# Graph layer and ternary feed-forward on one core: a lighter first stage, and shared node columns added by TensorE

## What is computed

```
n  = layernorm(x)
s  = segment_sum(n[src], dst, 1250);  deg = segment_sum(1, dst, 1250)
h  = n @ W_self + (s / max(deg, 1)) @ W_neigh + b
h  = where(h >= 0, h, 0.01 * h)
x  = x + h / max(norm(h, axis=1), 1e-12)
wq = w with each group of 128 inputs as clip(round(w / scale), -1, 1) * scale, scale = mean|w| + 1e-5
m  = layernorm(x)
x  = x + (silu(m @ wq_gate.T) * (m @ wq_up.T)) @ wq_down.T
```

## Time and profile before

| | |
|---|---|
| three runs | 363.98, 365.71, 365.72 us; median 365.71 |
| profiled execution | 365.24 us, span 363.3 us, mean granted clock 0.987 |
| busy (share of the span) | PE 329.8 (91%), DVE 304.6 (84%), ACT 238.0 (66%), POOL 163.1 (45%) |
| stage one | to 121.98 us |
| stage two | 121.98 to about 177 us |
| stage three | from there to the end |

### The profile page before, as it was taken

One profiled execution on the slowest core, in us unless ns is written; L12 is line 12 of the kernel. 1 busy time (PEld: TensorE's weight loads), 2 busy tenths in 40 slices (PEclk: granted clock), 3 DMA queues, 4 the chain that ended last, 5 costly groups with the idle time before them and its releaser, 6 DMA issues.

```text
span 363.3 us, 5834 instructions
## 1 busy us (share of the span) xinstructions
PE 329.8 (91%) x1623; PEld 249.6 (69%) x1623; DVE 304.6 (84%) x789; ACT 238.0 (66%) x637; POOL 163.1 (45%) x223
## 2 busy tenths in 40 slices
PE   1997879899999999999687999999999999999992
PEld 0443335554545578777476898989899898889991
DVE  3569999899889248999696998999999989999994
ACT  2155958899787136774656768668777678676670
POOL 7000000110010590110003466888788787799992
PEclk9999999999999999999988999999999999999998
DMA  7961322233232001200000000000000000000215
GB/s 226 291 159 33 86 58 78 68 88 87 59 82 79 3 3 35 74 22 2 0 1 2 0 3 0 3 0 0 2 3 2 0 0 3 0 3 0 73 44 169
DMA packets 9412, 16.69 MB, mean 46 GB/s; under 512 B 1062, under 2 KB 1886, under 8 KB 9378
## 3 DMA queue, kind: packets, MB, share of 16 engines
q1 hardware_dynamic: 9300, 16.21, 15.9%
q10 hardware_dynamic: 78, 0.08, 0.1%
HBM read 13.73 MB, written 2.56 MB: 45 GB/s over the span
## 4 chain that ended last, share of the span: by engine, by line
PE 58%; DVE 26%; ACT 10%; issue 3%; POOL 1%; DVEq 0%; ACTq 0%; POOLq 0%
PE bank L1320 39%; PE bank L1208 7%; PE bank L1250 5%; DVE tq_gu L901 4%; DVE hot_dst L1005 3%; ACT mag_early L690 3%; DVE tq_d L901 2%; DVE hot_src L996 2%; ACT a_t L742 2%; DVE bn L1061 2%; ACT hot_src L675 2%; DVE x_sb L1058 2%; DVE z L1040 1%; PE bank L1232 1%; PE bank L1156 1%
## 5 line engine op out<-in xcount | busy, mean ns | idle before, releaser
L1320 PE MATMUL bank<-x_hi,t_gu 128*128 128x378 f32 (+1 forms) x264 | 96.9, 367 | 3.6 <-DVE x_lo L1075 2.8
L1320 PE MATMUL bank<-x_lo,t_gu 128*128 128x378 f32 (+1 forms) x264 | 95.5, 362 | 0.0
L1208 PE MATMUL bank<-w_sb,xnT 128*125 128x512 f32 x160 | 86.9, 632 | 4.8 <-ACT z L725 4.1
L1114 DVE SCALAR_TENSOR_TENSOR g_acc<-bank,nscale,g_acc 128x378 f32<-128x378 f32 (+1 forms) x99 | 64.3, 650 | 12.1 <-PE bank L1320 10.8
L612 POOL TENSOR_SCALAR thr<-absum 128x4 f32<-128x4 f32 (+1 forms) x34 | 10.7, 315 | 121.5 <-ACT mag_early L690 97.2
L1114 DVE SCALAR_TENSOR_TENSOR u_acc<-bank,nscale,u_acc 128x378 f32<-128x378 f32 (+1 forms) x99 | 64.1, 647 | 0.0
L633 POOL TENSOR_TENSOR acc<-acc,d_one 128x378 f32<-128x378 f32 (+1 forms) x58 | 60.9, 1052 | 0.1
L643 POOL TENSOR_TENSOR hh<-sg,u_acc 128x378 f32<-128x378 f32 (+1 forms) x32 | 35.1, 1098 | 57.4 <-ACT sg L830 57.3
L1320 PEld LDWEIGHTS bank<-x_hi,t_gu 128*128 128x128 f32 x264 | 51.1, 193 | 8.1 <-DVE x_lo L1075 3.5
L1320 PEld LDWEIGHTS bank<-x_lo,t_gu 128*128 128x128 f32 x264 | 51.0, 193 | 3.6
L1167 PEld LDWEIGHTS bank<-hot_dst,hot_src 128*125 128x125 bf16 x157 | 20.8, 137 | 42.0 <-DVE hot_dst L1005 23.0
(11 more groups left out here) (136 smaller groups left out, 558.5 us busy)
## 6 DMA issues: line engine op xcount, KB each, us to landing
raw<-in_L_ffn_w_gate SPq DMA_DIRECT2D x11, 256.0 KB, 2.7
raw<-in_L_ffn_w_up SPq DMA_DIRECT2D x11, 256.0 KB, 2.6
out_x<-x_sb SPq DMA_DIRECT2D x10, 224.0 KB
raw<-in_L_ffn_w_down SPq DMA_DIRECT2D x8, 256.0 KB, 2.7
x_sb<-in_x SPq DMA_DIRECT2D x1, 1344.0 KB
w_sb<-in_L_gnn_W_neigh SPq DMA_DIRECT2D x1, 1024.0 KB, 6.0
w_sb<-in_L_gnn_W_self SPq DMA_DIRECT2D x1, 1024.0 KB, 7.3
raw<-in_L_ffn_w_down SPq DMA_DIRECT2D x4, 192.0 KB, 2.3
```

The lines of the kernel that those rows point to most:

```text
L1114: nc.vector.scalar_tensor_tensor(out=to, in0=bank_of(u, what)[:, 0:w], scalar=nscale[:, j:j + 1], in1=to, op0=ALU.mult, op1=ALU.add).then_ ...
L1208: last = nc.tensor.matmul(to[0:TP, :], xnT[:, t, k * TP:(k + 1) * TP], w_sb[:, k, half * D:(half + 1) * D], start=k == 0, stop=k == KD - 1)
L1320: last = nc.tensor.matmul(to, w, parts[h], start=h == 0, stop=h == 1)
```

## The change

- Stage one holds 18 loads (72 jobs) instead of 25; the other 16 (60 jobs) stand in stage two: five before the first neighbour sum, then 4, 3, 2 and 2 after tiles 0 to 3 (`PHASE`, `late_jobs`). In stage one ACT's magnitudes begin four slots later than before, and DVE's signs come four slots after that.
- The joins go. ACT copies a block's 50 columns, and at a block's end PE adds the shared column: it waits for the copy of the block before (`block_out`), and multiplies that column of `a_t` by the identity into column 0 of the block. PE loads the 32 base columns into registers for it (before, DVE did that). The one join of the last block stays.
- The bias is added by PE: ones times the bias in two parts (high and rest), as a ninth product of z. POOL's additions go.
- From tile 2 on ACT, not DVE, normalizes the rows.
- ACT spreads the source numbers over 32 columns into a table of its own, and DVE's compare reads them four times. DVE makes the chunk tables two slots ahead.
- `x1_low` comes one tile earlier.

```diff
+    LOADS1 = 18
+    PHASE = [5, 4, 3, 2, 2, 0, 0, 0, 0, 0]
...
-        LOADS1 = 2 * NF + 3
...
-        def down_jobs(n):
-
-            lo, hi = (LOADS1 + max(0, min(NL, 3 * i // 2)) for i in (n, n + 1))
-            return range(load_end[lo - 1], load_end[hi - 1])
+        def late_jobs(n):
+
+            lo = LOADS1 + sum(PHASE[:n])
+            return range(load_end[lo - 1], load_end[lo + PHASE[n] - 1])
...
-            for t in range(NT):
-                pool.wait_ge(z_out, t + 1)
-                nc.gpsimd.tensor_tensor(z[:, t, :], z[:, t, :], bias_b[0:TP, :], ALU.add).then_inc(z_done, 1)
...
-                nc.scalar.activation(hot_src[:, b % SBS, 0:n, 0:TP],
-                                     src_lo[:, SB * b:SB * b + n, None].to_broadcast([P, n, TP]), ACT.Copy).then_inc(src_wide, 1)
+                nc.scalar.activation(src_rep[:, b % SBS, 0:n, :],
+                                     src_lo[:, SB * b:SB * b + n, None].to_broadcast([P, n, REP]), ACT.Copy).then_inc(src_wide, 1)
...
+                if i == 0 and 1 <= t and t + 1 < NT:
+                    act.wait_ge(shifted, 1 if t + 1 < LN_GROUPS[3][0] else 2)
+                    act.wait_ge(xn_T, t)
+                    nc.scalar.activation(xn[0:TP, (t + 1) % 2, :], x_sb[:, t + 1, :], ACT.Identity, bias=shift0[0:TP, t + 1:t + 2],
+                                         scale=rs[0:TP, t + 1:t + 2]).then_inc(normed, 1)
...
-                            to, cols = a_t[:, :, 1:N][:, :, bass.ds(bases[k], WIN - 1)], slice(1, WIN)
+                            to, cols = a_t[:, :, bass.ds(bases[k], WIN)], slice(0, WIN)
...
+            for j in late_jobs(0):
+                abs_of(j)
             for n in range(NT):
...
-                for j in down_jobs(n):
-                    abs_of(j)
+                if n < NT - 1:
+                    for j in late_jobs(n + 1):
+                        abs_of(j)
...
-                    for c in chunks_in(slot + 1):
+                    for c in chunks_in(slot + 2):
...
-                            nc.vector.tensor_tensor(hot_src[:, b % SBS, 0:n, 0:TP], iota[:, None, 0:TP].to_broadcast([P, n, TP]),
-                                                    hot_src[:, b % SBS, 0:n, 0:TP], ALU.is_equal)
+                            nc.vector.tensor_tensor(
+                                hot_src[:, b % SBS, 0:n, :].rearrange("p n (a r) -> p n a r", r=REP),
+                                iota[:, None, 0:P].rearrange("p n (a r) -> p n a r", r=REP).to_broadcast([P, n, P // REP, REP]),
+                                src_rep[:, b % SBS, 0:n, None, :].to_broadcast([P, n, P // REP, REP]), ALU.is_equal)
...
-                for k in blocks_ending(slot - 2):
-                    if k:
-                        join(k)
+                if NB - 1 in blocks_ending(slot - 2):
+                    join_last()
...
+            for j in late_jobs(0):
+                ternary_of(j)
             for n in range(NT):
                 neighbour_sum(n)
...
-                if n >= 4:
-                    x1_low(n - 4)
-                for j in down_jobs(n - 1):
-                    ternary_of(j)
+                if n >= 3:
+                    x1_low(n - 3)
+                if n < NT - 1:
+                    for j in late_jobs(n + 1):
+                        ternary_of(j)
...
+                if c == last_chunk[k] and 0 < k < NB - 1:
+                    pe.wait_ge(block_out, k)
+                    nc.tensor.matmul(bank[k % 3][0:TP, 0:NT * WIN].rearrange("p (s d) -> p s d", d=WIN)[:, :, 0:1],
+                                     ident[0:TP, 0:TP], a_t[:, :, bass.ds(bases[k], 1)].bitcast(F32),
+                                     start=False, stop=True, skip_group_check=True).then_inc(block_done, 1)
...
+                if half and k == KD - 1:
+                    if t == 0:
+                        pe.wait_ge(bias_set, 2)
+                    last = nc.tensor.matmul(to[0:TP, :], ones_r[0:33, 0:1].to_broadcast([33, TP]), bias_r[0:33, :],
+                                            start=False, stop=True)
```

More of the change, by code:

```diff
@@ L256, in chunk_used @@
             k = window(c)[0]
-            return (block_done, k + 1) if c == last_chunk[k] else (hot_used, c + 1 - k)
+            alone = k in (0, NB - 1) and c == last_chunk[k]
+            return (block_done, k + 1) if alone else (hot_used, c + 1 - (k > 0))
         def blocks_ending(slot):
@@ L552, in _ @@
             load_x(3)
-            sp.dma_start(bias_b[:, :], bias.rearrange("(a n) -> a n", a=1).to_broadcast([P, D])).then_inc(bias_in, 16)
+            sp.wait_ge(zeroed, 4)
+            for r in (0, 32):
+                sp.dma_start(bias_f[r:r + 1, :], bias.rearrange("(a n) -> a n", a=1)).then_inc(bias_in, 16)
             for l, (w, n) in enumerate(loads):
@@ L589, in _ @@
             nc.gpsimd.memset(a_t[:, :, LASTB:N].bitcast(F32), 0.0).then_inc(zeroed, 1)
+            nc.gpsimd.memset(bias_f[:], 0.0).then_inc(zeroed, 1)
             nc.gpsimd.memset(base_f[:, 0:1], 0.0).then_inc(zeroed, 1)
@@ L729, in _ @@
                 if slot < SLOTS:
-                    for j in jobs_in(slot, 6):
+                    for j in jobs_in(slot, 10):
                         abs_of(j)
@@ L896, in reciprocals, with shift0_of @@
                 dve.wait_ge(rstd, i + 1)
+            def shift0_of(i):
+                a, b = LN_GROUPS[i]
+                nc.vector.scalar_tensor_tensor(out=shift0[0:TP, a:b], in0=mv[0:TP, a:b, 0], scalar=-1.0, in1=rs[0:TP, a:b],
+                                               op0=ALU.mult, op1=ALU.mult).then_inc(shifted, 1)
             def ternary_of(j):
@@ L982, in _ @@
                     reciprocals(3)
-                if i == 0 and 1 <= t and t + 1 < NT:
-                    normalize(t + 1)
+                    shift0_of(3)
                 if i == 2 and 1 <= t <= NT:
@@ L1005, in _ @@
                         nc.vector.tensor_scalar(to, numbers, key[:, c:c + 1], None, ALU.is_equal).then_inc(hot_made, 1)
-                if slot == FIRST + 2:
-                    dve.wait_ge(prep, 9)
-                    _, bases = nc.values_load_multi_w_load_instructions(
-                        base_i[0:1, :], engines=[dve.engine], min_val=0, max_val=LASTB,
-                        skip_runtime_bounds_check_because="base_f is clamped to 0..LASTB on the chip")
-                for k in blocks_ending(slot - 2):
-                    if k:
-                        join(k)
+                if NB - 1 in blocks_ending(slot - 2):
+                    join_last()
                 if slot == CHECK:
@@ L1020, in _ @@
                     any_outside = dve.value_load(flag[0:1, 0:1])
-                for j in jobs_in(slot, 10):
+                for j in jobs_in(slot - 4, 10):
                     ternary_of(j)
@@ L1169, in add_chunk @@
                                  hot_dst[:, c % HOT, 0:NT * (hi - lo)].rearrange("p (s d) -> p s d", d=hi - lo),
-                                 start=c == first_chunk[k], stop=c == last_chunk[k],
-                                 skip_group_check=True).then_inc(block_done if c == last_chunk[k] else hot_used, 1)
+                                 start=c == first_chunk[k], stop=c == last_chunk[k] and k in (0, NB - 1),
+                                 skip_group_check=True).then_inc(chunk_used(c)[0], 1)
+                if c == last_chunk[k] and 0 < k < NB - 1:
[3 more added lines that the diff above has]
+                                     start=False, stop=True, skip_group_check=True).then_inc(block_done, 1)
             pe.wait_ge(const_done, 11)
@@ L1188, in _ @@
                     pe.wait_ge(w_self_in, 16)
+                if slot == FIRST + 2:
+                    pe.wait_ge(prep, 9)
+                    _, bases = nc.values_load_multi_w_load_instructions(
+                        base_i[0:1, :], engines=[pe.engine], min_val=0, max_val=LASTB,
+                        skip_runtime_bounds_check_because="base_f is clamped to 0..LASTB on the chip")
                 if slot == 1:
@@ L1208, in _ @@
                 last = nc.tensor.matmul(to[0:TP, :], xnT[:, t, k * TP:(k + 1) * TP], w_sb[:, k, half * D:(half + 1) * D],
-                                        start=k == 0, stop=k == KD - 1)
+                                        start=k == 0, stop=not half and k == KD - 1)
+                if half and k == KD - 1:
[3 more added lines that the diff above has]
+                                            start=False, stop=True)
                 if k == KD - 1:
```

83 lines of the change are left out of this document (44 added, 39 removed).

## The result

| | before | the change |
|---|---|---|
| median | 365.62 us (4 runs) | 381.39 us (4 runs: 380.40 to 382.00) |
| ratio | | 1.044, 95% interval 1.040 to 1.048 |
| profiled execution, span | 365.24, 363.3 us | 380.40, 378.2 us |
| first neighbour product (T) | 121.98 us | 122.98 us |
| from there to the last transposes of stage two | 54.68 us | 68.58 us |

The account below looks back on a forecast made before the run. The prediction took TensorE to be the bound in both stages: 365.2 us + 1.3 before T + 13.8 of stands in stage two + 0.4 for the clock = 380.7 us, about 4% slower, range 371 to 389.

Parts of the forecast that it names:

- What bounds the kernel: Both stages: TensorE is the bound; before T, lightening DVE or ACT can win at most 9.4 us.
- The waits of stage one: TensorE's waits for DVE's tables and ACT's copies of z before T: 8.4 of 9.4 us credited as won.
- register load: Before T, TensorE loads 32 bases into registers: 0.8 us more, ends 0.1 and 1.2.
- Identity products: Before T, 30 fp32 products on TensorE at 0.22 us each: 6.6 us more, ends 3 and 15.
- Bias products: Before T, ten products of 512 columns on TensorE at a neighbour product's pitch, 0.23 us: 2.3 us more.
- Sum before T: All stage-one terms together, -8.4 + 6.6 + 2.3 + 0.8: T comes 1.3 us later.
- Source table: DVE's compare in stage one, reading a run of 32 four times: 0.70 us for 1024 elements, today's rate.
- The chain of stage two: After T, magnitudes, thresholds and signs precede DVE's early sums: first transposes of normalized rows at T + 30.5, last about T + 68.5.
- The stands: Stage two, TensorE idle 0.6, 7.9, 3.5 and 3.0 us, less 1.2 of today's waits: 13.8 us more.
- The clock: Stage two, TensorE's clock at 0.50 for a tile or so after the 7.9 us stand: 0.4 us, ends 0 and 2.
- The x_lo step: Feed-forward products in stage two: x_lo one tile earlier wins nothing, since the fourth product needs the same x_lo.
- POOL's additions: Stage two: DVE waited 4.9 us for POOL's ten bias additions, but TensorE was busy then, so removing them wins nothing.

Follow-up runs that it names:

- k3: The change without its ten bias products, POOL adding the bias one tile at a time between its thresholds: 377.28 us, 1.035 of the kernel before.
- k1: The kernel before with only the change's job table, and POOL's bias additions set between its early thresholds: 378.21 us, 1.036 of the kernel before.
- k10: The kernel before with ACT normalization, source table of 8 columns, tables two slots ahead, signs two slots behind magnitudes: 361.22 us, 0.991 of the kernel before.
- k11: k10 with the early magnitudes starting four slots later, signs still two slots behind them: 360.73 us, 0.988 of the kernel before.
- k4: The change without the 30 identity products and TensorE's register load, DVE joining the shared columns as before: 378.64 us, 1.039 of the kernel before.
- k9: The change with the old job table, source table of 8 columns, early signs two slots behind magnitudes, x_lo one tile later: 370.69 us, 1.017.
- k7: The change with its 16 late loads spread flat, two after each of tiles 0 to 7: 384.31 us, 1.055 of the kernel before.
- k8: k7's flat table with DVE's signs one tile behind ACT's magnitudes: 374.93 us, 1.029 of the kernel before.
- k6: The change with the bias product's ones written out as 33 x 125 elements instead of one repeated column: 382.03 us, 1.047 of the kernel before.
- k2: The change with the job table of before (25 loads early) and a source table of 8 columns: 374.49 us, 1.026 of the kernel before.
- k5: The change with the old job table, joins on DVE, bias on POOL between thresholds, source table of 8 columns: 374.09 us, 1.027 of the kernel before.

## Why the prediction was right

- **What bounds the kernel.** Stage one: right. Each step that took products from TensorE moved T (k3 by 4.5 us from the first chunk product), and steps that only lighten DVE and ACT won less than the 9.4 us (k1 2.1, k10 2.9, k11 4.4).
- **The waits of stage one.** I credited 8.4 of the 9.4; all went. The register load was 0.6 (I took 0.8).
- **Identity products.** 0.14 to 0.19 by the starts of the slots, up to 0.20 by k4: some 0.16, 4.8 us, where I had 0.22 and 6.6.
- **Bias products: the term that failed.** "At the pitch of a neighbour product, 0.23", 2.3 us in all, was 0.56 and 5.6 us by the starts. The nearest row had the columns but not the place: this product follows an fp32 projection, not another of its kind.
- **Sum before T: right by luck.** With what was measured, -9.4 + 4.8 + 5.6 + 0.6 = +1.6; T moved +1.0; I had +1.3. The bias products were 3.3 us dearer than forecast; the identity products were 1.8, the waits 1.0 and the registers 0.2 cheaper, which cancels it to 0.3. A term was missing too: the new zeroing of the bias rows on POOL (5.84 to 6.36) was costed at nothing, but DVE's first normalization beside it grew by 0.46 us, in every run with the bias products, and TensorE's first transposes began at 7.97 instead of 7.50 (rows in the last section). The eight records of the start took 0.39 us less in the change's execution (6.10 us), so T hides it.
- **Source table.** 684 ns for 1024 elements, where I took 0.70.
- **The chain of stage two.** In us after T, forecast and measured: signs of the first group done 8.9 and 9.1, second sum 17.4 and 17.8, third sum 26.2 and 26.7, first transposes 30.5 and 31.0, last ones 68.5 and 68.6. DVE's signs waited 7.9 us for thresholds up to the third sum (some 7). That the table makes the loss is shown by k1 and k9. That the loss is waiting between engines is shown by k7 against k8 for the flat table; the change's own table was not run with a tile of lag, and for it the waits for thresholds and the dates above speak.
- **The stands.** 0.6, 7.5, 1.0 and 2.9 us against 0.6, 7.9, 3.5 and 3.0. The second was smaller, because TensorE came to it later, at half clock: the 2.4 us of the clock fell into that stand as said (1.0 + 2.4 against 3.5), and the 0.4 that I added for the clock was not seen. The third ended with DVE's x_lo, not with ACT's xn as forecast; in k1 it ended with xn and was as long. Stands and the clock's 2.4 us make 0.6 + 7.5 + 1.0 + 2.9 - 1.2 + 2.4 = 13.2 of the 13.9; 0.3 is the wait for ACT's degree row, and 0.4 is not placed.
- **The clock.** In the change's profile only the first stand left a slow clock; the third (2.87 us) was followed by 1.00. In k1, k3 and k6 a third stand of 2.89, 2.89 and 2.87 us was followed by 0.73 (165:170), 0.75 (165:170) and 0.67 (170:175). So stands of nearly one length show both, and a slow clock there is worth some 1.5 us (a tile of 6.6 us instead of 5.1). The Trainium skill, page "TensorE: Matmul & The Clock Gate", section "HAM oscillation — how this bites in real kernels", makes a cold start hang on a gap that is long enough; that all three stands would count as such was my reading, and the trace bears it out, in the change, for the first alone.
- **The x_lo step**, costed at nothing: right here, where the normalization behind it waits for more. k2 against k9 shows it at 3.5 us with DVE as the bound.
- **POOL's additions**, nothing won: right. Stage two is 54.8 us with them (k10) and 54.65 without (k9).

## What to carry to other kernels

Count a job moved out of a bound stage with its whole chain (here magnitude, threshold, sign) at the place where it lands; where the chain is three engines long, put a tile of lag between its ends, or the next tile waits for all three. An engine that is the bound should not take over small work from an engine with slack: TensorE's waits were 9.4 us, the new products and registers cost about 11, and the bias products, half of that, replaced additions that TensorE did not wait for in stage two. Price a new product by a row at the same place in the instruction stream, not by one of the same size.

## What was not expected of the hardware

DVE's work can stand still while POOL adds the bias. In k3, two of DVE's tables took 1.56 us while POOL added (0.45 for two of the same form at 48.77):

```profile
50.99 1.56 DVE L1025 TENSOR_SCALAR hot_dst<-iota_w,key 128x200 bf16<-128x200 uint16 x2
51.20 1.27 POOL L630 TENSOR_TENSOR z<-z,bias_b 125x512 f32<-125x512 f32 x1
```

The second table ends with the addition. With the additions in stage one the mean of DVE's signs was 450 ns in k1 and 389 in k5 instead of 346, but only 359 in k3. The Trainium skill, page "SBUF — State Buffer", section "Who interferes with whom", says that DVE, in its two-port modes or with two inputs in SBUF, shares a pair of ports with GpSimd, and that where both need it one holds it for its whole instruction while the other blocks; the trace agrees in the rows above. It is a reason to leave these additions out of a stage in which DVE is short, as the kernel before does.

DVE's first normalization, beside POOL's zeroing of tables, shows the same. Before, and with the bias rows to zero (0.52 us more on POOL):

```profile
5.67 1.69 DVE L881 TENSOR_SCALAR xn<-x_sb,mv,rs 125x512 f32<-125x512 f32 x1
```

```profile
5.67 2.15 DVE L895 TENSOR_SCALAR xn<-x_sb,mv,rs 125x512 f32<-125x512 f32 x1
```

It ends with POOL's row of zeroings (7.41 us before, 7.87 in the change), where the mean of DVE's ten normalizations before is 0.66 us. That POOL holds it up is read from these rows, not tested.

And the bias product: 0.56 us for 512 columns behind an fp32 projection, where the same columns take 0.23 in a row of their kind. Why is open; k6 rules out the repeated column.
